# AdaLN block with small attention and FP6 feed-forward: the feed-forward gate moves from the weights to the sums

## The reference, cut to what matters

```
h = layernorm(x) * (1 + ca) + sa
x = x + ga * attention(h)            # only the first 16 rows of each batch differ from the bias bo
h = layernorm(x) * (1 + cb) + sb
xd = nearest FP6 grid value of h / scale, times scale   # one scale per 32 numbers of a row
wd = the same for the weight (512 x 512)
x = x + gb * (xd @ wd.T + bias)
```

## Time and profile before

| what | us |
|---|---|
| median of 3 runs (355.77 to 358.9) | 355.81 |
| the profiled execution's own time | 356.23 |
| its span in the trace | 354.4 |

### The profile page before, as it was taken

How to read it: one execution, slowest core, us unless ns; L and a number is a source line. 1 busy time by engine, 2 the same in 40 slices (tenths; PEclk the granted TensorE clock), 3 DMA queues, 4 the chain that set the end, 5 groups by cost and what they waited for, 6 DMA issues and landing times.

```text
span 354.4 us, 6297 instructions
## 1 busy us (share of the span) xinstructions
PE 320.6 (90%) x2247; PEld 241.4 (68%) x2247; DVE 282.9 (80%) x498; ACT 241.5 (68%) x541; POOL 238.3 (67%) x138
## 2 busy tenths in 40 slices
PE   7897997849999989998999999988999989997894
PEld 5113555638898777786788778766887768675683
DVE  4487869939938997969898879797878989989832
ACT  3349844585978798789788899885779897241410
POOL 2328959165876897999498989984999499701000
PEclk9899998998999999999999999999999999998999
DMA  6996899996497097957696969697939982011122
GB/s 183 394 405 254 302 256 206 252 378 196 75 218 200 5 239 204 225 167 201 183 238 270 241 128 263 193 232 132 292 115 153 229 194 90 31 57 61 74 105 89
DMA packets 23797, 68.51 MB, mean 193 GB/s; under 512 B 2467, under 2 KB 2596, under 8 KB 19798
## 3 DMA queue, kind: packets, MB, share of 16 engines
q1 hardware_dynamic: 16224, 53.40, 44.7%
q0 software_dynamic: 7392, 14.68, 25.8%
q10 hardware_dynamic: 150, 0.02, 0.1%
HBM read 50.96 MB, written 17.14 MB: 192 GB/s over the span
## 4 chain that ended last, share of the span: by engine, by line
PE 36%; DVE 28%; ACT 16%; issue 8%; POOL 6%; DMA 3%; SPq 1%; DVEq 0%; ACTq 0%; POOLq 0%
PE ps L752 6%; PE ps L753 6%; PE ps L757 6%; ACT U L505 4%; DVE Q L1242 4%; PE ps L663 3%; DVE XL L1199 3%; DVE amax L1223 3%; DVE DD L1249 3%; PE ps L735 3%; DMA X<-in_wmod 3%; ACT unused L518 3%; DVE X L1256 2%; ACT XH L467 2%; PE ps L837 2%
## 5 line engine op out<-in xcount | busy, mean ns | idle before, releaser
L752 PE MATMUL ps<-WH,XH 128*128 128x512 f32 x256 | 108.8, 425 | 6.9 <-DVE X L1256 4.6
L753 PE MATMUL ps<-WL,XH 128*128 128x512 f32 x256 | 103.0, 402 | 0.0
L390 POOL TENSOR_TENSOR U<-U,c_bc 128x1024 f32<-128x1024 f32 x31 | 76.4, 2466 | 33.5 <-ACT U L505 31.8
L399 POOL TENSOR_TENSOR U<-U,sb_bc 128x1024 f32<-128x1024 f32 x31 | 74.2, 2395 | 4.3
L1199 DVE TENSOR_TENSOR XL<-ps,XH 128x512 fp32r<-128x512 f32 x64 | 43.8, 684 | 39.2 <-ACT XH L467 37.7
L757 PE MATMUL ps<-WH,XL 128*128 128x512 f32 x256 | 68.8, 390 | 0.0
L505 ACT ACTIVATE U<-X,nmr,rstd 128x512 f32<-128x512 f32 x64 | 48.2, 808 | 30.1 <-DVE nmr L1216 27.7
L467 ACT ACTIVATE XH<-ps 128x512 fp32r<-128x512 f32 x64 | 37.5, 586 | 42.6 <-PE ps L735 42.5
L752 PEld LDWEIGHTS ps<-WH,XH 128*128 128x128 f32 x256 | 49.7, 194 | 18.1 <-DVE X L1256 6.3
L753 PEld LDWEIGHTS ps<-WL,XH 128*128 128x128 f32 x256 | 49.9, 195 | 9.7 <-issue 0.7
L757 PEld LDWEIGHTS ps<-WH,XL 128*128 128x128 f32 x256 | 48.5, 189 | 10.8
(11 more groups left out here) (232 smaller groups left out, 442.1 us busy)
## 6 DMA issues: line engine op xcount, KB each, us to landing
X<-in_x SPq DMA_DIRECT2D x16, 1024.0 KB, 7.7
out<-X SPq DMA_DIRECT2D x15, 1024.0 KB, 6.2
X<-mod_scratch POOLq DMA_DIRECT2D x14, 1024.0 KB, 13.8
X<-in_wmod SPq DMA_DIRECT2D x2, 1024.0 KB, 13.5
sb_bc<-mod_scratch SPq DMA_DIRECT2D x7, 256.0 KB, 12.9
c_bc<-mod_scratch SPq DMA_DIRECT2D x7, 256.0 KB, 12.0
gb_bc<-mod_scratch SPq DMA_DIRECT2D x6, 256.0 KB, 7.6
X<-in_wmod SPq DMA_DIRECT2D x2, 512.0 KB, 4.6
```

Of the source, the lines that this page charges most:

```text
L390: nc.gpsimd.tensor_tensor(a, a, spread(c_bc[:, b % 2, :]), ALU.mult).then_inc(u_done, 2 if g == 0 else 1)
L399: nc.gpsimd.tensor_tensor(a, a, spread(sb_bc[:, b % 2, :]), ALU.add).then_inc(h_done, 2 if g == 0 else 1)
L752: M(bank, XH[:, n % 2, r], WH[:, b % 2, k, :], start=k == 0, stop=False)
L753: M(bank, XH[:, n % 2, r], WL[:, b % 2, k, :], start=False, stop=False)
```

## The change

- WH, WL hold one set of weights, plain, split once before the loop. Gone are the scaled copies, Wb's plain weights, GpSimd's `scale_weights` and `scale_turned`, ScalarE's `scale_first_weights`, `weight_high` and `keep_plain` in slots, VectorE's `weight_low` in slots, TensorE's weight transposes in slots, G and `pick`.
- The bias stands in its product's bank before the matmuls: ScalarE copies it there (`preset`) at the end of its slot q for tile q+2; for the first three tiles one small matmul does it. All matmuls of a product then accumulate, and the 13th is gone.
- Products use three banks in turn (3, 4, 2). Product n waits for its preset, which waits for add n-3.
- VectorE multiplies the bank by the gate's row (`times_gate`) before it adds. Its slot order: gate of q-1, low part of q+1, add of q-1.
- The gate's row is loaded per batch into one of two buffers (`gb_in`), one DMA per batch as before.
- After group 3 GpSimd does both halves of `from_grid`, between its passes on the next group. DD has two buffers, so it waits for the group before the last; s32 holds both halves' scales.
- In the start, gb's rows, its column form and its row for batch 0 are worked out later, in TensorE's slot 0; first loads are in another order; sb's row for batch 0 comes from one broadcast of a finished row.
- The head's rows in the scratch are re-ordered so that one DMA per batch fetches them.

Cut to its core:

```diff
 # TensorE
-                for k in range(NC):
-                    M(bank, XH[:, n % 2, r], WH[:, b % 2, k, :], start=k == 0, stop=False)
-                    M(bank, XH[:, n % 2, r], WL[:, b % 2, k, :], start=False, stop=False)
...
-                M(bank, pick[:, b:b + 1].to_broadcast([P, P]), G[:], start=False, stop=True).then_inc(y_done, 1)
+                if n >= 3:
+                    pe.wait_ge(preset_done, n - 2)
...
+                    for k in range(NC):
+                        part(XH, WH, k)
+                        part(XH, WL, k)
+                pe.wait_ge(xl_done, n + 1)
+                for k in range(NC):
+                    m = part(XL, WH, k, n > 0 and k == NC - 1)
+                m.then_inc(y_done, 1)
...
-                if q in FOLDS and FOLDS[q][0] == 1:
-                    weight_turn(*FOLDS[q], W_BANK)
-                if q in PLAIN:
-                    weight_turn(2, PLAIN[q], W_BANK)
 # ScalarE
+            def preset(n):
+                act.wait_ge(o_done, n - 2)
+                A.copy(ps[:, Y_BANKS[n % 3], :], bias_bc[:]).then_inc(preset_done, 1)
...
-                if q - 1 in FOLDS:
-                    weight_high(*FOLDS[q - 1], W_BANK)
-                if q - 1 in PLAIN:
-                    keep_plain(PLAIN[q - 1])
                 if q == 0:
-                    for h in range(2):
-                        deviations(1, h)
-                    for h in range(2):
-                        normalise(1, h)
+                    normalise(1, 0)
+                    copy_columns(1)
+                    normalise(1, 1)
+                    act.wait_ge(gb_mm, 1)
+                    A.copy(gb_bc[:, 0, :], ps[:, GB_BANK, :]).then_inc(gb_first, 1)
...
+                if 3 <= q + 2 < LAST:
+                    preset(q + 2)
 # VectorE
+            def times_gate(n):
...
+                dve.wait_ge(y_done, n + 1)
...
+                bank = ps[:, Y_BANKS[n % 3], :]
+                TT(bank, bank, gb_bc[:, b % 2, :], ALU.mult).then_inc(scaled, 1)
...
             for q in range(LAST):
-                if q >= 1:
+                if q >= 2:
+                    times_gate(q - 1)
+                if 1 <= q < LAST - 1:
+                    low_part(q + 1)
+                if q >= 2:
                     add_tile(q - 1)
-                if q + 1 < LAST:
-                    low_part(q + 1)
-                if q - 1 in FOLDS:
-                    weight_low(*FOLDS[q - 1], W_BANK)
...
                 if (g := due(q, 3)) is not None and g > FILLING:
-                    from_grid(g, 0)
                     to_grid(g, 1)
 # GpSimd
             for g in range(1, GROUPS):
-                modulate(g)
+                times_c(g, 0)
+                plus_sb(g, 0)
+                times_c(g, 1)
                 if g - 1 > FILLING:
-                    from_grid(g - 1)
-                if g % 2 == 0 and g >= 4:
-                    scale_turned(g // 2)
+                    from_grid(g - 1, 0)
+                plus_sb(g, 1)
+                if g - 1 > FILLING:
+                    from_grid(g - 1, 1)
                 if g + 3 < GROUPS:
                     sum_by_dma(g + 3)
```

More of the change, by code:

```diff
@@ L24 @@
 XSLOTS = 6
-GBIAS, V, GB, GA, C, SB = range(6)
+V, GA, GBIAS, GB, C, SB = range(6)
 COLUMNS, ROWS = 4, 6
@@ L30, with build @@
 AFTER = BEGIN + 2 * PERIOD + 12
[L33 to L43, removed]
+def build(nc, x, xh, WqT, WkT, WvT, WoT, bo, lna, BDs, rows, columns, masks, w, bias, cT, wmod, ident, out):
     mod_dram = nc.dram_tensor("mod_scratch", (ROWS, B, D), F32, kind="Internal").ap()
@@ L127, in build @@
         Wv, Wk, Wo = early, late, early
[L128 removed]
+        mod_w = (X1[:, 3, :, :], X1[:, 4, :, :], X1[:, 5, :, :], U[:, 1, :, :], late[:], early[:])
         cH = hs[:].rearrange("p (k r) -> p k r", k=NC)
         gate_rows = [msp[0:B, n, :] for n in (0, 1)]
[L132 removed]
+        column_rows = [msp[0:2 * B, n, :] for n in (2, 1)]
         sb_rows, c_rows_all = msp[0:B, 3, :], msp[0:B, 0, :]
         bo_bc, gate_tmp = att[:], odd[:]
[L135 to L137 removed]
         gate_sign = sb("gate_sign", [P, NC * B])
@@ L173, in build @@
         sb_in = [sem(f"sb_in{i}") for i in range(2)]
+        gb_in = [sem(f"gb_in{i}") for i in range(2)]
         wmod_in = [sem(f"wmod_in{i}") for i in range(7)]
@@ L443, in _ @@
                     centre_diagonals()
-            from_grid(GROUPS - 1)
+            for h in range(2):
+                from_grid(GROUPS - 1, h)
         @block.scalar
@@ L670, in gate_columns, with turn_columns @@
                 m.then_inc(gate_mm, 1)
+            def turn_columns(i):
+                pe.wait_ge(gates_done, i + 1)
+                for n in range(NC):
+                    m = TR(ps[0:2 * B, COLUMN_ROWS[i], n * P:(n + 1) * P],
+                           TA[:, n, 2 * i:2 * i + 2, :].rearrange("p w b -> p (w b)"), idf[:])
+                m.then_inc(rows_turned, 1)
             def head_rows(i, bank):
@@ new lines, in product, with part @@
+            def product(n):
+                bank = ps[:, Y_BANKS[n % 3], :]
+                if n >= 3:
+                    pe.wait_ge(preset_done, n - 2)
+                pe.wait_ge(xh_done, n + 1)
+                def part(a, w, k, last=False):
+                    return M(bank, a[:, n % 2, k * P:(k + 1) * P], w[:, k, :], start=False, stop=last,
+                             skip_group_check=n >= 3)
+                if n == 0:
+                    for k in range(NC):
+                        part(XH, WH, k)
+                else:
+                    for k in range(NC):
+                        part(XH, WH, k)
+                        part(XH, WL, k)
@@ L754, in product @@
                 pe.wait_ge(xl_done, n + 1)
                 for k in range(NC):
-                    r = slice(k * P, (k + 1) * P)
-                    M(bank, XL[:, n % 2, r], WH[:, b % 2, k, :], start=False, stop=False)
+                    m = part(XL, WH, k, n > 0 and k == NC - 1)
                 if n == 0:
-                    pe.wait_ge(g_rows, 4)
-                M(bank, pick[:, b:b + 1].to_broadcast([P, P]), G[:], start=False, stop=True).then_inc(y_done, 1)
+                    for k in range(NC):
+                        pe.wait_ge(wt_low, k + 1)
+                        m = part(XH, WL, k, k == NC - 1)
@@ L1269, in _ @@
             first_times_c()
-            gate(1, GB, BIAS, GBIAS, gb_col)
             first_plus_sb()
@@ L1276, in _ @@
             from_grid(0, 0)
-            for k in range(NC):
-                weight_low(0, k, W_FIRST_BANKS[k])
+            weight_low(0)
             low_part(0)
-            gate_bias_rows()
+            for k in range(1, NC):
+                weight_low(k)
             maxima(0, 1)
+            gate(1, GB, BIAS, GBIAS, gates_done)
+            scales(1)
+            low_part(1)
             block_scales(0, 1, 2)
```

443 lines of the change are left out of this document (198 added, 245 removed).

## The result

The changed kernel takes 360.25 us in the median, the kernel before 356.97 beside it on the same chips: ratio 1.0092, 95% interval 1.0065 to 1.0118. I had forecast 345 us with the range 335 to 356, so the direction was wrong. The change costs 0.9%. The profiled executions are 357.79 us (span 355.9) and 356.23 (span 354.4), a difference of 1.6 us; 1% is 3.6 us in all that follows.

The account below looks back on a forecast made before the run. It took TensorE as nearest to a bound, at 92% of the steady part, VectorE second. Terms -2.2, -9.5 and +0.7 us sum to -11.0, giving a forecast of 345 us, range 335 to 356.

Parts of the forecast that it names:

- -2.2 for the start: Start to product 11: slots 7 to 10 save 2.7 us on TensorE, small new pieces cost 0.5.
- -9.5 for products 11 to 62: 51 tiles of the loop: TensorE's saving less 1 us more stalls gives -4.5 us per 24 tiles, -9.5 in all.
- +0.7 for the end: After the last product, VectorE does gate and add instead of add alone: 0.7 us more.
- The price of TensorE's work: TensorE's bias matmul goes: 0.228 us a tile, 14.6 us over 64 tiles, saved where TensorE sets the time.
- In light slots it costs nothing: VectorE's gate multiply fills its idle time before the low part; in heavy slots it costs 0.6 to 0.7 us.
- Mostly hidden: ScalarE's wait for VectorE's add before the preset is mostly covered by group work; uncovered, up to 0.6 us a slot.
- The third bank: TensorE's product banks: the 4.6 us of bank waits should go in part, to waits for XL.
- rival B: GpSimd brings from_grid's first half too late for TensorE's transposes in 12 groups: slower, 361 us, chance 0.10.
- A: VectorE sets the pace, so TensorE's saving becomes idle time: 352.5 to 354 us, say 353.5, chance 0.14.
- C: Third bank and lighter start give more; stalls fall to 5 us in 24 tiles: 334 us, chance 0.12.
- Wrong altogether: Sign against the whole prediction: the 24 steady tiles taking above 105 us, where about 101 was expected.
- the clock is not the subject: TensorE's granted clock read as 0.9 to 1.0 in every slice, 2.4 GHz apart from short breaks; no time given to it.

Follow-up runs that it names:

- scales early: VectorE's three small scale instructions per group moved ahead of the next tile's low part: ratio 0.9916 on the changed kernel, 0.9843 on the kernel before.
- all three orders: Changed kernel with VectorE's scales ahead of the low part, add ahead of the low part, preset behind the next high part: 0.9751 against the kernel before.

## Why the prediction was wrong

The sum had three terms, -2.2 for the start, -9.5 for products 11 to 62 and +0.7 for the end. Start and end came out at -3.1 and +1.2, and product 0 ended at 37.5 us (forecast 38 to 40), product 11 at 115.2 (about 116). The step that failed is the middle one: "TensorE loses 0.228 x 24 = 5.5 us in each 24 tiles: 97.6 to 92.1 ... I expect stalls to grow from 8 to 9 ... -4.5 in 24 tiles". The work fell by just that, and the stalls grew from 8 to 15.4, so the 24 tiles took 107.5 us and not 101.1. Measured for products 11 to 62: +3.4 instead of -9.5.

**The price of TensorE's work.** I took TensorE for the bound because it was at 92% of the steady part, and gave each of its microseconds its full price, less one. (Second in busy time was GpSimd with 91.2 us, not VectorE with 90.2.) Taken away alone they are worth 3.1 us of 14.6, and 1.2 with the scales early. At 92, 85, 86 and 83% I read this as no bound at all, only engines that wait in turn, where a stall of one is set by the order on another. What a microsecond of an engine's work is worth depends on the kernel that it stands in and on its place there. In pairs of kernels that differ by that work: TensorE's matmul 3.1 of 14.6, 7.2 of 13.9, and with all three orders 9.7; VectorE's multiply 9.3 of 44.2 in the change, 19.7 of 44 in the kernel before; VectorE's half 10.7 of 14.5 (GpSimd's 23 us go the other way); ScalarE's preset 2.6 of 35.4. Each pair can be read as work added or as work taken away, so these numbers give no rule that the one pays less than the other costs.

**The gate.** "In light slots it costs nothing" rested on 37.7 us of idle before the low part. I then expected that idle to fall under 20 us, and it rose to 44.2. But this does not show that the idle can't be filled. Much of VectorE's other work went with the same change (21.9 us of weights, 14.5 of halves), and without the gate the wait is 72.4 us. The gate took 28.5 us of it. What the reading missed is the rest: the sum has no term of its own for the gate in heavy slots, only 1 us more of stalls in 24 tiles, and none for the chain that XH hangs on (VectorE's scales behind the gate, ScalarE's normalise, the high part). The gate costs 9.3 us, nearly the size of the whole gain forecast for the loop.

**The preset.** "Mostly hidden" holds for its work: taken out whole, with its place, it gives back 2.6 us of 35.4, and its place ahead of the high part alone accounts for 2.5. It waits 33.7 us for the add, and low part before add puts a low part of 0.69 us ahead of that add, which is worth 2.5 in its run. These numbers overlap: with the preset gone altogether no more than 2.6 came back.

**The third bank.** It was to take some of 4.6 us of bank waits. These went, and the preset's (9.0 us on the weight loads, before 6.3 for the add) and XH's came (7.8 for 0.9). I had named XL as what would be late next; it was XH (XL made TensorE wait 2.6). No run tried the third bank alone.

**GpSimd.** Its half took 1.915 us (forecast 1.913), and the transposes waited for GpSimd 0.4 us in all, where over 10 would have been rival B. B had the right sign and the nearest time (361), for a mechanism that did not happen. The Trainium skill's ratio of 1.96 (GPSIMD Engine Reference, Performance versus the Vector engine) does not hold for this pass: 1915 ns against 1219 ns for the same shape on VectorE in the kernel after is 1.57. The page's row is an add of fp32 to fp32, and for two fp32 inputs the kernel before agrees with it: 2395 ns on GpSimd (L399) against 1226 on VectorE (L994, the same shape) is 1.95. The page's advice, to keep such work on VectorE, would have cost 10.7 us here.

**Rivals A and C.** A is the nearest in mechanism: VectorE's chain eats TensorE's saving. Its sum let stalls take the saving up and no more; it gave the gate no price. It was also added up wrongly: -3.5 from 355.8 or 356.2 is 352.3 to 352.7, not 353.5. C is refuted: stalls grew. Wrong altogether would be, I wrote, a steady part above 105 us; it is 107.5.

**The clock.** I put it at nothing ("the clock is not the subject") after reading 0.9 to 1.0 in every slice; in the earlier trace rows four of the 40 slices show an 8. Between products 11 and 62 the kernel after ran 13.6 us at the lower clock, the kernel before 3.4. By the rows of the last section that is about 3.8 us of TensorE's time, an estimate, where the loop grew by 3.4. It is no separate cause as far as is seen, since the falls follow waits, and the kernel in all three orders has as much of it (13.6 us) and is 7 us shorter in this stretch (224.6 us). How much of the loss it carries was not tried.

**A count of the parts.** By the runs on the changed kernel: TensorE's bias matmul gone about -7.2 by adding it (-3.1 by taking it from the kernel before), presets with their place +2.6, gate +9.3, halves -10.7, low part ahead of the add +2.5. With -3.1 this gives +0.6, where +3.3 was measured. With -7.2 it gives -3.5. The parts were tried from different kernels and overlap, and the weight parts, 21.9 us of VectorE's work that went, were not tried alone. How the 3.3 us divide stays open.

## What to carry to other kernels

Where four engines stand within 10% of each other and hand a tile round, price an edit by what it does to the latest hand-over, not by the busy time. Here a microsecond of work was worth between 0.07 (ScalarE's presets) and 0.74 (VectorE's halves), and the engine that looked nearest to a bound gave 0.21. Try the main term of a forecast alone on the kernel before: that one run would have shown 3.1 us where 14.6 were counted. Idle time before an instruction can be filled, but not at no cost: here it took about 28 of 44 us, and 9 showed. To see what went into it compare with and without that one piece of work, not before and after the whole change. And before judging such a change, re-order each engine's slot, in both kernels: three moves turned +0.9% into -2.5% (-2.0% by all executions), but the largest of them gives the kernel before nearly as much.

## What was not expected of the hardware

TensorE's clock fell after its own waits. Timeline of the kernel after, the product behind a wait, and the window before it (columns as above):

```profile
121.73 0.76 PE L717 MATMUL ps<-WH,XH 128*128 128x512 f32 x1 [1.89 <-ACT XH L447]
122.30 0.63 PE L717 MATMUL ps<-WL,XH 128*128 128x512 f32 x1
...
124.43 0.58 PE L717 MATMUL ps<-WH,XH 128*128 128x512 f32 x1
124.85 0.39 PE L717 MATMUL ps<-WL,XH 128*128 128x512 f32 x1
```

```profile
118.50:121.50 3.00, 0.63 (x4) 0.42 (x4) 2.97 (x6) 3.00 (x9) 1.98 (x1) 0.99 0.90 140
```

TensorE had worked 0.63 us of the 3.0 before; then it ran at 0.50, the 1.2 GHz level, and a matmul took 0.43 us from start to start instead of 0.23. All stretches at the lower clock between products 11 and 62, first in the kernel after, then in the kernel before:

```profile
121.40:124.80 3.40, 3.07 (x7) 2.48 (x8) 3.19 (x7) 3.40 (x10) 3.26 (x3) 0.50 1.05 148
234.10:237.50 3.40, 3.40 (x10) 2.63 (x9) 3.40 (x6) 2.65 (x7) 3.40 (x2) 0.51 0.31 82
326.20:333.00 6.80, 4.62 (x15) 4.05 (x16) 5.98 (x12) 1.60 (x3) 1.61 (x1) 0.50 0.00 0
```

```profile
322.90:326.30 3.40, 3.40 (x8) 2.73 (x9) 3.40 (x5) 0.59 (x1) 0.00 (x0) 0.50 0.00 0
```

TensorE worked 11.1 of these 13.6 us, before 3.4 of 3.4. At half the rate that is 5.5 us lost against 1.7, an estimate. Counted by product matmuls over 0.55 us in the loop, there are 22 in the kernel after and 7 in the kernel before; the 15 more, at 0.2 us each, are 3 us. It is not only the profiled execution: the mean granted clock was 0.95 in the median of the 20 executions of the kernel after, and 0.98 in the 82 of the kernel before beside the other runs. So a wait can cost more than its own length. That the falls follow from the waits was read from where they stand (in the 3 us before each fall TensorE had worked 0.7, 1.7 and 1.2 us, before 1.0), and no run tried it alone.

The other surprise is how little TensorE's work was worth when taken away alone from the kernel before, 3.1 of 14.6 us.
